# Attention stage: the low f16 half of the transposed normalised rows made by VectorE from PSUM instead of by GpSimd from an SBUF copy

## What is computed

```python
x = x + xattn(layernorm(x), ctx, tgt_mask, src_mask, Wq, Wk, Wv, Wo, bo)
x = x + ffn(layernorm(x), gate_w, w1, b1, w2, b2, sw1, sb1, sw2, sb2)

# xattn
q, k, v = heads(x @ Wq.T), heads(ctx @ Wk.T), heads(ctx @ Wv.T)
sim = where(mask, q @ k.T * 64**-0.5, -big)
out = (softmax(sim) @ v) @ Wo.T + bo
```

## Time and profile before

| | us |
|---|---|
| median of 3 runs | 1998.26 (1997.72 to 2003.76) |
| the profiled execution | 1997.06, its span 1995.3 |
| stage of the folded matrices | 0 to about 98 |
| start of the attention pipeline | 98 to 140 |
| attention, written out, then loop | 140 to 227, 227 to 477 |
| end of attention | 477 to 517 |
| shared and routed nets | 517 to 1995 |

### The profile page before, as it was taken

The page is one execution under the profiler, slowest core; times in us unless marked ns, Lnnn a source line. Parts: engine busy times, 40 slices in busy tenths (PEclk is TensorE's granted clock), DMA queues, the critical chain, the costliest instruction groups (busy, mean ns, idle before and its releaser), DMA issues. The chain is left out here.

```text
span 1995.3 us, 32828 instructions
## 1 busy us (share of the span) xinstructions
PE 1884.6 (94%) x11964; PEld 1202.5 (60%) x11965; DVE 887.6 (44%) x1668; ACT 848.3 (43%) x1506; POOL 520.6 (26%) x635
## 2 busy tenths in 40 slices
PE   8889999999899999999999999999989798989997
PEld 6344444444566666666666665666656565656664
DVE  6989888889343333333333333222222222222222
ACT  4644444444334444444444443334334243333333
POOL 1068888887100001000001002111211111212111
PEclk9999999999999999999999999999999899999998
DMA  9145555554822222222222526111110111111100
GB/s 322 65 141 172 173 170 171 170 166 152 301 76 75 93 88 95 94 74 74 82 97 91 193 97 251 35 33 34 43 35 30 31 34 31 33 34 44 43 18 15
DMA packets 123641, 198.20 MB, mean 99 GB/s; under 512 B 20208, under 2 KB 61680, under 8 KB 123120
## 3 DMA queue, kind: packets, MB, share of 16 engines
q1 hardware_dynamic: 115584, 171.01, 25.7%
q0 software_dynamic: 7920, 25.17, 3.9%
HBM read 137.95 MB, written 58.98 MB: 99 GB/s over the span
## 5 line engine op out<-in xcount | busy, mean ns | idle before, releaser
L1024 DVE TENSOR_TENSOR room_a<-room_a 128x256 f16<-128x256 f32 (+1 forms) x528 | 233.6, 443 | 935.9 <-ACT room_a L1011 931.9
L978 PE MATMUL pH<-room_a,room_f 128*128 128x256 f16 x4608 | 572.4, 275 | 34.7 <-issue 29.4
L990 PE MATMUL pY<-room_f,room_a 128*128 128x512 f16 x2304 | 559.6, 380 | 4.6 <-DVE room_a L1024 4.6
L978 PEld LDWEIGHTS pH<-room_a,room_f 128*128 128x128 f16 x4608 | 454.8, 99 | 165.3 <-issue 39.5
L1009 ACT ACTIVATE room_a<-pH,e_bsel,sc 128x256 f32<-128x256 f32 (+1 forms) x272 | 151.6, 557 | 454.3 <-PE pH L978 432.4
L990 PEld LDWEIGHTS pY<-room_f,room_a 128*128 128x128 f16 x2304 | 225.6, 98 | 197.4 <-DVE room_a L1024 4.9
L1009 ACT ACTIVATE room_a<-pH,b1s,sc 128x256 f32<-128x256 f32 x256 | 144.2, 563 | 365.2 <-PE pH L978 364.5
L978 PE MATMUL pH<-room_a,room_v 128*128 128x256 f16 (+1 forms) x1728 | 202.7, 269 | 14.8 <-issue 14.5
L1171 POOL TENSOR_TENSOR room_a<-room_a,s_brow 128x512 f32<-128x512 f32 x32 | 42.4, 1344 | 617.6 <-DVE room_a L1032 617.6
L978 PEld LDWEIGHTS pH<-room_a,room_v 128*128 128x128 f16 x1728 | 162.7, 99 | 64.8 <-issue 19.1
L990 PE MATMUL pY<-room_v,room_a 128*128 128x512 f16 x816 | 198.1, 379 | 0.0
(11 more groups left out here) (191 smaller groups left out, 1785.5 us busy)
## 6 DMA issues: line engine op xcount, KB each, us to landing
room_b<-in_w SPq DMA_DIRECT2D x64, 256.0 KB, 4.3
s_er<-in_w SPq DMA_DIRECT2D x32, 512.0 KB, 6.5
rows_room<-in_x SPq DMA_DIRECT2D x32, 256.0 KB, 4.5
room_a<-in_sw SPq DMA_DIRECT2D x32, 256.0 KB, 4.8
room_b<-in_x SPq DMA_DIRECT2D x32, 256.0 KB, 2.8
s_split<-room_a SPq DMA_DIRECT2D x64, 128.0 KB, 4.2
x_scratch<-room_b SPq DMA_DIRECT2D x32, 256.0 KB, 3.0
z_scratch<-room_b SPq DMA_DIRECT2D x32, 256.0 KB, 3.4
```

Of the source, the lines that this page charges most:

```text
L978: mm = q.matmul(self.pH[j % 2][:, 0:rows], w[:, k, j * P:(j + 1) * P], zt[:, u, k, 0:rows], start=(n == 0), stop=(n == 3 * KC - 1))
L990: mm = q.matmul(self.pY[u][r][:, :], h[:, j % self.HR, r * P:(r + 1) * P], w[:, j, :], start=(j == 0 and n == 0), stop=(j == HC - 1 and n ...
L1024: q.tensor_tensor(self.hl[:, j % self.HR, 0:rows], self.hf[:, j % self.HR, 0:rows], self.hh[:, j % self.HR, 0:rows], ALU.subtract).then_in ...
```

## The change

The float32 copy `xTf` and ScalarE's read that made it go away. The low half is made by VectorE, in one instruction that reads `pX` and `xTh`, scales, subtracts and writes f16. On VectorE it stands between `gate` and `largest_w`, in the body of the same tile as before; for the first tile it stands after the constants, ahead of the first body. On GpSimd nothing stands in its place. The transposes of the next tile wait for the low half, since that is now the last reader of `pX`.

```diff
-                xTf = take([KC, P])
...
                         def t_x(e, g, u):
                             e.wait_ge(S["xn"], count(g, u))
-                            at_least(e, S["xTh"], count(g, u) - 1)
+                            at_least(e, S["xTl"], count(g, u) - 1)
...
                         def hi_x(e, g, u):
                             e.wait_ge(S["xT"], count(g, u))
-                            at_least(e, S["xTl"], count(g, u) - 1)
-                            e.activation(xTf, pX[:, :].rearrange("p (k n) -> p k n", k=KC), ACT.Copy, scale=LN_SCALE)
+                            at_least(e, S["xTl"], count(g, u) - 2)
                             at_least(e, S["sim"], count(g, u) - 2)
...
-                        def lo_x(e, g, u):
-                            e.wait_ge(S["xTh"], count(g, u))
-                            e.tensor_tensor(xTl[:, u % 2, :, :], xTf, xTh[:, u % 2, :, :], ALU.subtract).then_inc(S["xTl"], 1)
...
-                        lo_x(pool, 0, 0)
...
                                 step(pool, g, u, 1, norm)
-                                if not first_tile(g, u, 3):
-                                    step(pool, g, u, 3, lo_x)
                                 step(pool, g, u, 0, add_bo)
...
+                        def lo_x(e, g, u):
+                            e.wait_ge(S["xTh"], count(g, u))
+                            at_least(e, S["sim"], count(g, u) - 2)
+                            e.scalar_tensor_tensor(out=xTl[:, u % 2, :, :], in0=pX[:, :].rearrange("p (k n) -> p k n", k=KC), scalar=LN_SCALE,
+                                                   in1=xTh[:, u % 2, :, :], op0=ALU.mult, op1=ALU.subtract).then_inc(S["xTl"], 1)
...
                         dve.wait_ge(S["src_neg"], 2)
+                        lo_x(dve, 0, 0)
...
                                 step(dve, g, u, -1, gate)
+                                if not first_tile(g, u, 3):
+                                    step(dve, g, u, 3, lo_x)
                                 step(dve, g, u, 2, largest_w)
```

## The result

| | us |
|---|---|
| before, median of 7 executions | 1998.26 (1997.33 to 2003.76) |
| changed, median of 7 executions | 2006.12 (2003.29 to 2007.74) |
| ratio | 1.0032, 95% interval 1.0021 to 1.0044 |
| profiled execution, changed | 2006.68, its span 2004.9 (before: 1997.06, 1995.3) |

The changed kernel was slower, as forecast, and inside the range, but by 8 us between the medians and 9.6 us between the profiled executions, where 13.8 were worked out. And this is not the whole result: measured twice more, the same program gave 1994.5 us against 2002.1 for the kernel before (ratio 0.9969, interval 0.9957 to 0.9981), and then executions at 1994 and at 2006 on one chip (2004.8 in the median, ratio 1.0037, interval 1.0024 to 1.0051). That the first set came out slower, as forecast, was so in part luck. The experiments came to that only at the end, so the first profile is read first.

What follows compares the result with a forecast made beforehand. Attention steps were taken as paced by the VectorE and GpSimd chain from residual to residual, TensorE close behind. 1997.06 us profiled + 11.1 (steps) + 2.7 (start) = 2010.9, for the median 2012 us; range 1990 to 2023.

Steps and rivals of the forecast that it cites:

- three orders: Attention steps sorted by whether VectorE's gate loses to GpSimd's normalisation, precedes it, or precedes the last small row-scale operation.
- B: Steps where VectorE's gate loses to GpSimd's normalisation, 18 of 28; claimed +0.7 us each.
- C: Steps where VectorE's gate precedes the last small operation of GpSimd's row scales, 5 of 28; claimed +0.6 us each.
- A: Steps where VectorE's gate goes before GpSimd's normalisation, 5 of 28; claimed -0.9 us each, with a margin of 0.15 us.
- The end of amw: VectorE's 128x2 maximum, gate-loses steps: claimed to end with GpSimd's subtraction of the maximum, at 460.4 for 459.72 us.
- Pick and residual are behind it: +0.7: VectorE, gate-loses steps: operations queued behind the 128x2 maximum move with its end, step +0.7 us (+0.4 to +0.9).
- The start: First three tiles: subtraction queued behind other VectorE work, scores +1.5, +2.3, then some +0.4 more; +2.7 us taken (1.5 to 4.4).
- the rival in which the gate wins more often: VectorE's gate wins everywhere in the loop, or everywhere: -8 us (1990) or -20 us (1978), faster; chance 0.10.
- its partial form: Half or three in four of twenty loop steps become gate-first: +7 or 0 us, no change; chance 0.15.
- The exclusion: VectorE instructions with two SBUF inputs and GpSimd ones reading SBUF hold each other up; new subtraction, 0.69 us, never stretched.

Runs made afterwards that it cites:

- the scalar forms: 128x2 maximum made as two 128x1 operations with a per-partition scalar each: on the changed kernel 1988.46 us, on the kernel before 1997.30 us.
- the stand-in: Changed kernel with GpSimd doing an unused operation of the same form and size where its subtraction stood: 2000.07 us, ratio 1.0013.
- the run with the mask row later: Kernel before the change with VectorE's mask row put behind the row statistics: 1995.77 us, ratio 0.9967.
- the kernel with the gate moved: Changed kernel with 128x2 maximum as two scalar operations, gate ahead of the scores' maximum, new subtraction behind the weight maxima: 1980.34 us, ratio 0.9912.
- with the other start as well: Same edits on the changed kernel, plus first subtraction ahead of the constants' wait, next three between masked scores and their maximum: 1976.28 us, ratio 0.9894.

## Why the prediction was right and wrong

**What bounds, and the mechanism: right.** The three orders, their counts (18, 5, 5) and their places in the loop were in the first changed profile just as in the kernel before. In B and C amw was behind sub, in A in front of it. The kernel with the scalar forms and the one with the stand-in show from two sides that this is what lengthens B and C.

**The size of a step: this is the part that failed.** Said +0.7, +0.6 and -0.9 us for B, C and A, measured +0.47, +0.29 and -1.11. The end of amw was right: 8.02 us after the aggregation in B, 0.75 later than before. The step of the reasoning that failed is the one behind it, "Pick and residual are behind it: +0.7": it took the shift of amw's end for the shift of the residual, and that for the shift of the next aggregation. Two things lie on that way. In most of the written-out B steps the residual was indeed 0.71 us later (8.06 for 7.35), but behind it comes the mask row, which has two SBUF inputs as well and which in the kernel before met GpSimd's operation 658. With the residual later, the row misses that meeting, and 0.24 us come back; the run with the mask row later shows the hold-up by itself. In the B steps of the loop that meeting had cost at most 0.07 us. There the residual was only 0.50 to 0.55 us later (8.06 for 7.51 and 7.56), because I carried over the 0.25 us between the end of amw and the residual of the earlier trace rows; they were 0.05 us once amw ended later, in C too. In A the residual came 1.01 us earlier, and the mask row, held up 0.1 us less, gave the rest of the 1.11. Together the 28 steps gave +4.2 for +11.1.

**The start: too small.** Said +2.7, with 1.5 to 4.4 for bounds, measured +4.8. The order of the waits was as written, but the first scores came 0.5 us later and not 1.5, and I took the matmul groups at the speeds of the kernel before. Two more of the three ran at 7.03 us, 3.4 us together. The changed kernel was also measured at 141.98 us (5.34, 6.77, 5.35), so part of the 4.8 is that execution's and not the change's.

**A margin taken for a fact.** "Nothing ahead of gate or norm within a step changes, and the written-out part was B each time" was the case against the rival in which the gate wins more often, and I gave that and its partial form 0.25. True as far as it goes, but 0.03 us of dispatch is no margin. With amw in front of sub in such a step, a won race is now worth 12.85 - 11.39 = 1.46 us; in the kernel before it cost 0.12 (12.50 for 12.38, with the scalar forms). So the change raised the price of a race that the kernel before could afford, and the answer to "faster or slower" depends on the execution: 2003 to 2008 us where the gate loses, 1993 to 2000 where it wins every second time, as far as the three profiles tell, against 1996 to 2005 before.

**The exclusion.** It holds in every row shown here: two SBUF inputs against GpSimd are held up, and the new subtraction, one input from PSUM, took 0.68 to 0.70 us in all 32 tiles, whatever GpSimd did, as the Trainium skill has it (SBUF - State Buffer, Who interferes with whom). On the order, the recorded starts alone mislead: a gate recorded first still lost unless it was 39 ns or more ahead. In rows rounded to 0.01 us even that can't be seen, since the 0.04 us of the stand-in (184.52 against 184.56, lost) are 32 ns and the 0.04 us of 157.32 against 157.36 (won) are 44.

## What to carry to other kernels

Before moving work from one engine to another, list the instructions of both that exclude each other, however small, and lay both streams over each other after the move: what gets earlier may get in front of something that matters, and a hold-up that was hidden may come into the open. Where such a meeting can't be ordered by a margin of 0.1 us or more (0.11 was enough here every time), change the form (one tensor and a per-partition scalar) or the place, so that there is no race; the kernel with the gate moved spread over 0.8 us in five executions (with the other start as well, 4.5 us in four), the changed kernel over 14 us in seven. And measure a change of this kind with many executions and on more than one chip.

## What was not expected of the hardware

- The same program went two ways, by 10 us, in executions on one chip, and the profiles that show both ways differ by a race of two engines dispatched 0.02 to 0.05 us apart: 39 ns ahead won every time, 37 ns lost every time.
- A 128x1 operation with one SBUF tensor and a per-partition scalar from SBUF ran in 0.21 us beside a GpSimd operation with two SBUF inputs; the 128x2 operation with two SBUF tensors took up to 1.59 us in the steps of order C.
- The time of the first score groups (24 matmuls in 5.34 us, or in 7.03 us, with a mean granted clock of 0.66 over the 5 us from 106.0 in the first changed profile, so at the lower of its two levels, 1.2 GHz, for part of it) differed at the same idle time of 3.39 us ahead of the first group: 7.03 in the first and third changed profile, 5.34 in the second. The idle time there doesn't settle it.
